# Attention stage of a four-layer pipeline: row sums from the exponentials' accumulator output, and weighing in pairs of rows

## The chip, the cores and the metric

The kernel runs on one core of one Trainium2 chip. The core has five engines, each with a queue of its own that runs in order: TensorE (PE in the profile; PEld is its weight load), VectorE (DVE), ScalarE (ACT), GpSimd (POOL) and SyncE (SP, which here only starts transfers). They meet at semaphores alone. The metric is the time of one execution on the device in microseconds.

## The reference

The input is x, an image of 256 rows x 256 columns x 128 channels. Four layers follow, each with a group normalization ahead. Only the first, attention along each row of the image, is touched:

```
q = split_heads(gn(x) @ Wq) / sqrt(32);  k, v = split_heads(kv_x @ Wk), split_heads(kv_x @ Wv)
a = softmax(einsum('bnhqc,bnhkc->bnhqk', q, k) + mask_bias + tri_bias)      # 4 heads of 32 channels
o = einsum('bnhqk,bnhkc->bnhqc', a, v) * sigmoid(gn(x) @ Wg)
x = x + o @ Wo
```

Here n is the image row, and q and k run over its 256 columns. So there are 256 independent attentions, each with 4 heads and scores of 256 x 256. A Fourier layer, a convolution layer and a gated layer with large kernels follow.

## The kernel before

`attention` writes the whole stage as one block with a queue for each engine. All 256 rows are unrolled. In iteration n the queues work on different rows at once, and the order inside an iteration is written out by hand (the loops `for n in range(-2, rows + 2)` at the end of each engine's part). Each buffer is guarded by waits on counting semaphores.

For a row, with its 256 columns as two halves of 128:

- TensorE turns the row's x and kv_x by transposes into `p_in` (`turn`, L328). VectorE reads them out with the normalization applied (`read_turn`, L511, L512).
- TensorE makes queries and keys (`project_qk`, L333, L334), ScalarE reads them (`read_qk`). Then it makes values and gate (`project_vg`, L339, L341), and ScalarE reads the values and the exponential of minus the gate (`read_vg`, L448, L449). All four steps share the one bank `p_in`.
- TensorE makes the scores (`score`, L350), the four heads in four row groups of the array. VectorE adds the bias and finds the maximum (`add_bias`, L478), ScalarE takes the exponentials (`exps`, L427) into `probs`. The bias, `tri` plus the row's mask, is added by GpSimd (`add_mask`, L309).
- The exponentials are turned by 128x128 transposes (`turn_probs`, L361) into two banks. Heads 0 and 2 use `p_t[0]`, which VectorE reads (L486); heads 1 and 3 use `p_t[1]`, which ScalarE reads (L419). Both go to `probs_t`.
- The softmax's denominator is a column sum of the turned exponentials. GpSimd adds the two halves of the keys (`pair`, L301), and TensorE multiplies the result by a matrix of ones, head by head in the four column groups of the array, so that each sum comes out on all 32 channels of its head (L376). The values are weighed in the same column groups (L373). Together they are `weigh`.
- VectorE multiplies the sums by one plus the gate's exponential (`denominator`, L493). ScalarE inverts that by Ln and then Exp of the negative (`invert`, L433, L435). VectorE multiplies it with the weighed values (`gate`, L500), TensorE projects (`project_out`, L383), VectorE adds x (`residual`, L506), and SP stores the row.

`weigh`, `denominator`, `invert`, `gate`, `project_out` and `residual` of row n - 2 run in iteration n, each once a row. On TensorE `weigh` stands between `project_vg(n + 1)` and the transposes of head 0. On VectorE `gate` stands ahead of `add_bias(n + 1, 0)`, and `residual` between `add_bias(n + 1, 1)` and `add_bias(n + 1, 2)`. On ScalarE `invert` stands behind the exponentials of heads 1 to 3.

Of the kernel before, what the change touches and what calls it, by code (L numbers as in the profile page):

```python
# [202 lines left out]
def attention(nc, x, kv, tri_bias, mask_bias, wq, wk, wv, wg, wo, ident, scale, shift, x1, rows=ROWS):  # L203
# [7 lines left out]
    maskv = mask_bias[0].rearrange("r a b k -> r (a b) k")  # L211
    with ExitStack() as ctx:
# [3 lines left out]
        ones = m.sb("ones", [128, HEAD_DIM])  # L216
# [3 lines left out]
        xs = m.sb("xs", [128, 8, HALVES, CH])  # L220
        kvs = m.sb("kvs", [128, 8, HALVES, CH])
# [4 lines left out]
        vs = m.sb("vs", [128, 4, HALVES, CH])  # L226
        gate_e = m.sb("gate_e", [128, 4, COLS])
        den = m.sb("den", [128, 2, COLS])
# [3 lines left out]
        probs_t = m.sb("probs_t", [128, 3, HEADS, HALVES, COLS])  # L232
        paired_t = m.sb("paired_t", [128, 2, HEADS, COLS])
        og = m.sb("og", [128, 2, COLS])
# [7 lines left out]
        const_loaded, cleared = m.sem("const_loaded"), m.sem("cleared")  # L242
        x_loaded = [m.sem(f"x_loaded{i}") for i in range(8)]
        kv_loaded = [m.sem(f"kv_loaded{i}") for i in range(8)]
        mask_loaded = [m.sem(f"mask_loaded{i}") for i in range(4)]
        x1_stored = [m.sem(f"x1_stored{i}") for i in range(4)]
# [3 lines left out]
        p_turned, even_read, odd_read, paired = (m.sem(n) for n in ("p_turned", "even_read", "odd_read", "paired"))  # L250
        weighed, den_made, den_step, gated = (m.sem(n) for n in ("weighed", "den_made", "den_step", "gated"))
# [5 lines left out]

        @block.sync
        def _(sp):
            def load(n):  # L260
                if n >= 8:
                    sp.wait_ge(x1_made, n - 7)
                    sp.wait_ge(turned, n - 7)
                sp.dma_start(xs[:, n % 8], xv[n]).then_inc(x_loaded[n % 8], 16)
                sp.dma_start(kvs[:, n % 8], kvv[n]).then_inc(kv_loaded[n % 8], 16)
# [13 lines left out]
            for n in range(-2, rows + 2):  # L279
                if n + 4 < rows:  # L280
                    load(n + 4)
                if n + 4 < rows:
                    load_mask(n + 4)
                if exists(n - 2):
                    sp.wait_ge(x1_made, n - 1)
                    sp.dma_start(x1v[n - 2], x1s[:, (n - 2) % 4]).then_inc(x1_stored[(n - 2) % 4], 16)
            for p in range(4):
                sp.wait_ge(x1_stored[p], 16 * (rows // 4))

        @block.gpsimd  # L290
        def _(pool):
            pool.memset(ones[:, :], 1.0).then_inc(cleared, 1)
            pool.wait_ge(const_loaded, 16 * 6)

            def pair(n, half):
                pool.wait_ge(even_read, 2 * n + half + 1)
                pool.wait_ge(odd_read, 2 * n + half + 1)
                if n >= 2:
                    pool.wait_ge(weighed, n - 1)
                part = slice(2 * half, 2 * half + 2)  # L300
                pool.tensor_tensor(paired_t[:, n % 2, part], probs_t[:, n % 3, part, 0], probs_t[:, n % 3, part, 1],  # L301
                                   ALU.add).then_inc(paired, 1)
# [9 lines left out]
            for n in range(-2, rows + 2):  # L312
                for half in range(2):
                    if exists(n - 1):
                        pair(n - 1, half)
                    if exists(n + 2):
                        add_mask(n + 2, half)

        @block.tensor
        def _(pe):  # L320
            def turn(n):
                pe.wait_ge(x_loaded[n % 8], 16 * (n // 8 + 1))
                pe.wait_ge(kv_loaded[n % 8], 16 * (n // 8 + 1))
                if n >= 1:
                    pe.wait_ge(vg_read, n)
                for i, src in enumerate((xs, kvs)):
                    for half in range(HALVES):
                        mm = pe.transpose(p_in[:, i, half * 128:(half + 1) * 128], src[:, n % 8, half, :], ident[:, :])  # L328
                mm.then_inc(turned, 1)
# [25 lines left out]
            def turn_probs(n, h):  # L355
                pe.wait_ge(exped, n * HEADS + h + 1)
                if n >= 1 or h >= 2:
                    pe.wait_ge((even_read, odd_read)[h % 2], n * 2 + h // 2)
                for kh in range(HALVES):
                    for qh in range(HALVES):  # L360
                        mm = pe.transpose(p_t[h % 2][:, kh, qh * 128:(qh + 1) * 128],  # L361
                                          probs[:, h, qh, kh * 128:(kh + 1) * 128], ident[:, :])
                mm.then_inc(p_turned, 1)

            def weigh(n):
                pe.wait_ge(paired, 2 * n + 2)
                pe.wait_ge(vg_read, n + 1)
                if n >= 1:
                    pe.wait_ge(x1_made, n)
                for kh in range(HALVES):  # L370
                    for h in range(HEADS):
                        ch = slice(HEAD_DIM * h, HEAD_DIM * (h + 1))
                        pe.matmul(p_out[ch, 0, :], vs[:, n % 4, kh, ch], probs_t[:, n % 3, h, kh, :],  # L373
                                  start=kh == 0, stop=kh == HALVES - 1)
                for h in range(HEADS):
                    mm = pe.matmul(p_out[HEAD_DIM * h:HEAD_DIM * (h + 1), 1, :], ones[:, :], paired_t[:, n % 2, h, :],  # L376
                                   start=True, stop=True)
                mm.then_inc(weighed, 1)

            def project_out(n):  # L380
                pe.wait_ge(gated, n + 1)
                for half in range(HALVES):
                    mm = pe.matmul(p_out[:, 0, half * 128:(half + 1) * 128], og[:, n % 2, half * 128:(half + 1) * 128], wo_s,  # L383
                                   start=True, stop=True)
# [3 lines left out]
            pe.wait_ge(cleared, 1)  # L388
            for n in range(-2, rows + 2):
                if exists(n + 1):  # L390
                    project_vg(n + 1)
                if exists(n - 2):
                    weigh(n - 2)
# [12 lines left out]
                if exists(n - 2):  # L406
                    project_out(n - 2)
                if exists(n):
                    turn_probs(n, 3)

        @block.scalar
        def _(act):
            act.preload_act_table_set(EXP_LN_SET)

            def read_probs(n, h):
                act.wait_ge(p_turned, n * HEADS + h + 1)
                if n >= 3:
                    act.wait_ge(weighed, n - 2)
                act.activation(probs_t[:, n % 3, h], p_t[1][:, :, :], ACT.Copy).then_inc(odd_read, 1)  # L419

            def exps(n, h):
                act.wait_ge(biased, n * HEADS + h + 1)
                if n >= 1:
                    act.wait_ge(p_turned, (n - 1) * HEADS + h + 1)
                for qh in range(HALVES):
                    i = h * HALVES + qh
                    e = act.activation(probs[:, h, qh, :], neg_s[:, n % 2, h, qh, :], ACT.Exp,  # L427
                                       bias=neg_max[:, n % 2, i:i + 1], scale=-1.0)
                e.then_inc(exped, 1)

            def invert(n):
                act.wait_ge(den_made, n + 1)
                act.activation(den[:, n % 2], den[:, n % 2], ACT.Ln).then_inc(den_step, 1)  # L433
                act.wait_ge(den_step, 2 * n + 1)
                act.activation(den[:, n % 2], den[:, n % 2], ACT.Exp, scale=-1.0).then_inc(den_step, 1)  # L435
# [8 lines left out]
            def read_vg(n):  # L444
                act.wait_ge(vg_made, n + 1)
                if n >= 4:
                    act.wait_ge(den_made, n - 3)
                act.activation(vs[:, n % 4], p_in[:, 0, :], ACT.Copy)  # L448
                act.activation(gate_e[:, n % 4], p_in[:, 1, :], ACT.Exp, scale=-1.0).then_inc(vg_read, 1)  # L449

            for n in range(-2, rows + 2):
# [6 lines left out]
                if exists(n - 2):  # L458
                    invert(n - 2)
# [10 lines left out]
        def _(dve):  # L470
# [11 lines left out]
            def read_probs(n, h):  # L482
                dve.wait_ge(p_turned, n * HEADS + h + 1)
                if n >= 3:
                    dve.wait_ge(weighed, n - 2)
                dve.tensor_copy(probs_t[:, n % 3, h], p_t[0][:, :, :]).then_inc(even_read, 1)  # L486

            def denominator(n):
                dve.wait_ge(weighed, n + 1)
                dve.wait_ge(vg_read, n + 1)  # L490
                if n >= 2:
                    dve.wait_ge(gated, n - 1)
                dve.scalar_tensor_tensor(out=den[:, n % 2], in0=gate_e[:, n % 4], scalar=1.0, in1=p_out[:, 1, :],  # L493
                                         op0=ALU.add, op1=ALU.mult).then_inc(den_made, 1)

            def gate(n):
                dve.wait_ge(den_step, 2 * n + 2)
                if n >= 2:
                    dve.wait_ge(out_made, n - 1)
                dve.tensor_tensor(og[:, n % 2], p_out[:, 0, :], den[:, n % 2], ALU.mult).then_inc(gated, 1)  # L500

            def residual(n):
                dve.wait_ge(out_made, n + 1)
                if n >= 4:
                    dve.wait_ge(x1_stored[n % 4], 16 * (n // 4))
                dve.tensor_tensor(x1s[:, n % 4].rearrange("p h c -> p (h c)"), p_out[:, 0, :],  # L506
                                  xs[:, n % 8].rearrange("p h c -> p (h c)"), ALU.add).then_inc(x1_made, 1)
# [6 lines left out]
            for n in range(-2, rows + 2):  # L514
                if exists(n - 2):
                    denominator(n - 2)
# [4 lines left out]
                if exists(n - 2):  # L521
# [1723 lines left out]
```

## Time and profile before

| what | value |
|---|---|
| median of 3 executions | 4797.06 us (4793.52 to 4877.1) |
| profiled execution | 4796.05 us |
| its span, first to last instruction | 4793.8 us |
| mean granted TensorE clock | 0.958 of 2.4 GHz |
| TensorE busy | 4411.2 us, 92% of the span |
| VectorE busy | 3431.3 us, 72% |
| ScalarE busy | 2804.1 us, 58% |
| GpSimd busy | 2614.8 us, 55% |

Attention runs from about 112 to about 1985 us of the span. A row of a timeline gives the start, the time from the start of its first instruction to the end of its last, the engine, the line, the operation, output and inputs by the program's names, and how many instructions were merged in it. A bracket at its end says how long the engine was idle before it and what released it. On TensorE the ends are modelled and neighbours overlap, so the distance from one start to the next tells more than a duration. A matmul of fp32 counts as two instructions. In a row of the table of stretches stand the stretch, its length, the busy time of PE, PEld, DVE, ACT and POOL with their instructions in brackets, the granted TensorE clock as a share of 2.4 GHz, the share of DMA time and GB/s.

### The profile page before, as it was taken

The numbers are of one execution on the slowest core, as the hardware profiler recorded it, in microseconds if no ns is written. First come the engines' busy times: TensorE is split into PE (matmuls) and PEld (weight loads), VectorE is DVE, ScalarE is ACT, GpSimd is POOL, SyncE is SP. The second block draws the span as 40 slices with busy tenths as digits, with TensorE's granted clock in tenths as the row PEclk, the third lists the DMA queues.
The fourth block names the chain that finished last, engine by engine and source line by source line (L and its number), as shares of the span: only waits on it lengthen the run. The fifth ranks groups of instructions, "written<-read, shape, count | busy, mean of one in ns | idle before, by whom it ended". The sixth has DMA issues, their size and how long they took to land. (4 is left out here: it accounts for less than half of the span.)

```text
span 4793.8 us, 108030 instructions
## 1 busy us (share of the span) xinstructions
PE 4411.2 (92%) x36006; PEld 3297.2 (69%) x36006; DVE 3431.3 (72%) x10053; ACT 2804.1 (58%) x6302; POOL 2614.8 (55%) x2043
## 2 busy tenths in 40 slices
PE   5999999999999999777899989999749997999996
PEld 5777777777777777534577766777424445999995
DVE  7888888888888888651566666666429995567666
ACT  0888888888888888402333343333325662666665
POOL 0999999999999999402233322333105551122222
PEclk8999999999999999887999999999869998999997
DMA  7222222222222222597322222222567887999995
GB/s 311 63 77 73 75 74 74 75 74 76 75 75 75 73 75 74 187 381 248 104 71 73 71 84 71 73 71 73 223 220 214 277 278 245 264 292 293 291 291 137
DMA packets 803939, 713.02 MB, mean 149 GB/s; under 512 B 60693, under 2 KB 700948, under 8 KB 794839
## 3 DMA queue, kind: packets, MB, share of 16 engines
q1 hardware_dynamic: 784875, 672.74, 45.8%
q10 hardware_dynamic: 14717, 20.01, 1.2%
q0 software_dynamic: 3808, 13.47, 0.7%
q8 instruction: 292, 4.78, 0.4%
q14 instruction: 247, 2.02, 0.1%
HBM read 506.70 MB, written 199.29 MB: 147 GB/s over the span
## 5 line engine op out<-in xcount | busy, mean ns | idle before, releaser
L309 POOL TENSOR_TENSOR at_bias<-at_tri,at_mask 128x1024 f32<-128x1024 f32 x512 | 1216.0, 2375 | 27.9 <-DMA at_mask<-in_L_conv_mask_bias_dram 12.1
L427 ACT ACTIVATE at_probs<-at_neg_s,at_neg_max 128x256 f32<-128x256 f32 x2048 | 871.4, 505 | 0.7 <-DVE at_neg_max L478 0.7
L478 DVE CUSTOM_DVE_ANT_0 at_neg_s<-at_p_s,at_bias 128x256 f32<-128x256 f32 x2048 | 759.8, 418 | 7.6 <-PE at_p_s L350 2.9
L301 POOL TENSOR_TENSOR at_paired_t<-at_probs_t 128x512 f32<-128x512 f32 x512 | 655.9, 1281 | 9.7 <-ACT at_probs_t L419 5.6
L361 PE MATMUL at_p_t<-all_ident,at_probs 128*128 128x128 f32 x4096 | 628.3, 276 | 0.6 <-DVE at_probs_t L486 0.4
L969 ACT ACTIVATE ml_h<-ml_p_turns,l_b 128x512 f32<-128x512 f32 x384 | 263.8, 687 | 607.2 <-PE ml_p_turns L928 607.2
L361 PEld LDWEIGHTS at_p_t<-all_ident,at_probs 128*128 128x128 f32 x4096 | 476.0, 141 | 131.7 <-issue 104.1
L1070 POOL TENSOR_TENSOR ml_x2t<-ml_z,ml_xb 128x512 f32<-128x512 f32 x128 | 163.7, 1279 | 675.1 <-DVE ml_z L1036 675.1
L937 PEld LDWEIGHTS ml_p<-l_w1s,ml_h 128*128 128x128 f32 x4096 | 471.9, 192 | 52.7 <-issue 52.7
L1990 POOL TENSOR_TENSOR dw_room<-dw_room,all_b_plain 128x512 f32<-128x512 f32 x128 | 176.9, 1382 | 589.1 <-DMA dw_room<-x3t 589.1
L928 PE MATMUL ml_p_turns<-ml_h,l_w 128*128 128x512 f32 x1024 | 485.3, 597 | 2.3 <-DVE ml_h L1002 2.3
L937 PE MATMUL ml_p<-l_w1s,ml_h 128*128 128x128 f32 x4096 | 484.6, 277 | 0.8 <-issue 0.8
L486 DVE COPY at_probs_t<-at_p_t 128x512 f32<-128x512 f32 x512 | 352.6, 689 | 36.0 <-PE at_p_t L361 1.5
L2023 DVE SCALAR_TENSOR_TENSOR dw_hid<-dw_room 128x512 f32<-128x512 f32 x128 | 154.4, 1206 | 207.8 <-ACT dw_room L1919 207.8
L419 ACT ACTIVATE at_probs_t<-at_p_t 128x512 f32<-128x512 f32 x512 | 300.2, 586 | 1.2 <-PE at_p_t L361 1.2
L350 PE MATMUL at_p_s<-at_keys,at_queries 32*128 32x256 f32 x4096 | 294.3, 401 | 0.0
L373 PE MATMUL at_p_out<-at_probs_t,at_vs 128*32 128x256 f32 x4096 | 274.2, 385 | 1.4 <-DVE at_x1s L506 1.4
L1008 DVE TENSOR_SCALAR ml_h<-ml_p_turns,l_b 128x512 f32<-128x512 f32 x128 | 96.0, 750 | 244.4 <-PE ml_p L937 242.0
L928 PEld LDWEIGHTS ml_p_turns<-ml_h,l_w 128*128 128x128 f32 x1024 | 176.2, 192 | 132.4 <-issue 127.6
L1817 PE MATMUL dw_p_conv<-dw_xw,all_kept 128*128 128x128 f32 x2048 | 253.4, 276 | 9.9 <-DMA dw_xw<-planes 5.8
L1817 PEld LDWEIGHTS dw_p_conv<-dw_xw,all_kept 128*128 128x128 f32 x2048 | 244.3, 192 | 10.5 <-DMA dw_xw<-planes 5.9
L1817 PE MATMUL dw_p_conv<-dw_xw,dw_wts 128*128 128x128 f32 x2048 | 250.8, 274 | 0.0
(230 smaller groups left out, 9110.2 us busy)
## 6 DMA issues: line engine op xcount, KB each, us to landing
dw_xw<-planes SPq DMA_DIRECT2D x128, 528.0 KB, 4.7
sp_xs<-x SPq DMA_DIRECT2D x128, 512.0 KB, 9.1
dw_wts<-patch_w SPq DMA_DIRECT2D x128, 512.0 KB, 6.2
planes<-pw_plane SPq DMA_DIRECT2D x128, 264.0 KB, 3.2
in_xs<-in_x_dram SPq DMA_DIRECT2D x32, 1024.0 KB, 7.7
at_xs<-in_x_dram SPq DMA_DIRECT2D x256, 128.0 KB, 2.5
at_kvs<-in_L_conv_kv_x_dram SPq DMA_DIRECT2D x256, 128.0 KB, 2.7
at_mask<-in_L_conv_mask_bias_dram SPq DMA_DIRECT2D x256, 128.0 KB, 3.3
```

What stands on the lines that cost most here:

```text
L301: pool.tensor_tensor(paired_t[:, n % 2, part], probs_t[:, n % 3, part, 0], probs_t[:, n % 3, part, 1], ALU.add).then_inc(paired, 1)
L309: pool.tensor_tensor(bias[:, n % 2, part], tri[:, part], mask[:, n % 4].unsqueeze(1).broadcast_to((128, 4, COLS)), ALU.add).then_inc(maske ...
L350: mm = pe.matmul(p_s[h][:, qh, :], queries[ch, n % 2, qh * 128:(qh + 1) * 128], keys[ch, n % 2, :], start=True, stop=True)
L361: mm = pe.transpose(p_t[h % 2][:, kh, qh * 128:(qh + 1) * 128], probs[:, h, qh, kh * 128:(kh + 1) * 128], ident[:, :])
L373: pe.matmul(p_out[ch, 0, :], vs[:, n % 4, kh, ch], probs_t[:, n % 3, h, kh, :], start=kh == 0, stop=kh == HALVES - 1)
L419: act.activation(probs_t[:, n % 3, h], p_t[1][:, :, :], ACT.Copy).then_inc(odd_read, 1)
L427: e = act.activation(probs[:, h, qh, :], neg_s[:, n % 2, h, qh, :], ACT.Exp, bias=neg_max[:, n % 2, i:i + 1], scale=-1.0)
L478: t = dve.tensor_tensor_reduce(neg_s[:, n % 2, h, qh, :], p_s[h][:, qh, :], bias[:, n % 2, i, :], -1.0, 3.0e38, ALU.add, ALU.min, neg_max[ ...
L486: dve.tensor_copy(probs_t[:, n % 3, h], p_t[0][:, :, :]).then_inc(even_read, 1)
L928: mm = pe.matmul(bank_of(hidden_use(t, b))[:, :], w0[:, b * 128:(b + 1) * 128], h[:, t % 2, :], start=True, stop=True)
L937: mm = pe.matmul(p_2[:, j, :], h1[:, b, j * 128:(j + 1) * 128], w1c[:, b, :], start=b == 0, stop=b == blocks - 1)
L1817: mm = pe.matmul(p_conv[g % 2][:, j, :], weights, xw[:, k % 3, :, g % 2 * 4 + j, side:side + PX], start=side == 0, stop=side == 1)
```

## The change

- The exponentials get an accumulator output, which leaves each query's sum in `sums` (queries on partitions). GpSimd spreads a row's sums over the 32 channels of each head (`spread_sums`), and for two rows at a time TensorE transposes them (`turn_sums`) into `p_t[0]`. `pair`, `paired_t`, `ones` and the ones matmuls go.
- `weigh`, `denominator`, `invert`, `gate`, `project_out` and `residual` handle two rows q = (2q, 2q + 1) in one visit. `pair_at(n, lag)` gives the pair that is due in iteration n: the denominator, weighing, inversion and gate at lag 3 (odd n), the output projection and the residual at lag 4 (even n), the store at lag 5, `turn_sums` at lag 2 (even n).
- `p_out` holds weighed values of two rows in its two halves. Buffers get deeper: `xs` and `kvs` 10 rows, `vs` and `gate_e` 6, `probs_t` 4, `den` and `og` two pairs.

```diff
+    held, pairs = 10, rows // 2
...
+        def pair_at(n, lag):
+            return (n - lag) // 2 if n % 2 == lag % 2 and lag <= n < rows + lag else None
...  gpsimd
-            def pair(n, half):
-                ...
-                pool.tensor_tensor(paired_t[:, n % 2, part], probs_t[:, n % 3, part, 0], probs_t[:, n % 3, part, 1],
-                                   ALU.add).then_inc(paired, 1)
+            def spread_sums(n):
+                pool.wait_ge(exped, (n + 1) * HEADS)
+                if n >= 4:
+                    pool.wait_ge(sums_turned, (n - 4) // 2 + 1)
+                pool.tensor_copy(spread[:, n % 4], sums[:, n % 4].unsqueeze(3).broadcast_to((128, HALVES, HEADS, HEAD_DIM))
+                                 ).then_inc(sums_spread, 1)
...
             for n in range(-2, rows + 2):
-                for half in range(2):
-                    if exists(n - 1):
-                        pair(n - 1, half)
-                    if exists(n + 2):
-                        add_mask(n + 2, half)
+                if exists(n + 2):
+                    add_mask(n + 2, 0)
+                if exists(n - 1):
+                    spread_sums(n - 1)
+                if exists(n + 2):
+                    add_mask(n + 2, 1)
...  tensor, turn_probs
+                if h == 0 and n >= 3:
+                    pe.wait_ge(den_made, (n - 1) // 2)
...
+            def turn_sums(q):
+                pe.wait_ge(sums_spread, 2 * q + 2)
+                pe.wait_ge(even_read, min(4 * q + 6, 2 * rows))
+                for r in range(2):
+                    for half in range(HALVES):
+                        mm = pe.transpose(p_t[0][:, r, half * 128:(half + 1) * 128],
+                                          spread[:, (2 * q + r) % 4, half].rearrange("p h d -> p (h d)"), ident[:, :])
+                mm.then_inc(sums_turned, 1)
+
+            def weigh(q):
+                pe.wait_ge(even_read, 4 * q + 4)
+                pe.wait_ge(odd_read, 4 * q + 4)
+                pe.wait_ge(vg_read, 2 * q + 2)
+                if q >= 1:
+                    pe.wait_ge(x1_made, q)
+                for r in range(2):
+                    n = 2 * q + r
+                    for kh in range(HALVES):
+                        for h in range(HEADS):
+                            ch = slice(HEAD_DIM * h, HEAD_DIM * (h + 1))
+                            mm = pe.matmul(p_out[ch, r, :], vs[:, n % 6, kh, ch], probs_t[:, n % 4, h, kh, :],
+                                           start=kh == 0, stop=kh == HALVES - 1)
                 mm.then_inc(weighed, 1)
...
-            for n in range(-2, rows + 2):
+            for n in range(-2, rows + 3):
                 if exists(n + 1):
                     project_vg(n + 1)
-                if exists(n - 2):
-                    weigh(n - 2)
+                q = pair_at(n, 3)
+                if q is not None:
+                    weigh(q)
                 if exists(n):
                     turn_probs(n, 0)
...
                 if exists(n):
                     turn_probs(n, 2)
-                if exists(n - 2):
-                    project_out(n - 2)
+                q = pair_at(n, 4)
+                if q is not None:
+                    project_out(q)
                 if exists(n):
                     turn_probs(n, 3)
+                q = pair_at(n, 2)
+                if q is not None:
+                    turn_sums(q)
...  scalar, exps
                     e = act.activation(probs[:, h, qh, :], neg_s[:, n % 2, h, qh, :], ACT.Exp,
-                                       bias=neg_max[:, n % 2, i:i + 1], scale=-1.0)
+                                       bias=neg_max[:, n % 2, i:i + 1], scale=-1.0,
+                                       accum_out=sums[:, n % 4, qh, h:h + 1])
...  vector
+                dve.scalar_tensor_tensor(out=den[:, q % 2], in0=gate_e[:, 2 * q % 6:2 * q % 6 + 2], scalar=1.0, in1=p_t[0][:, :, :],
+                                         op0=ALU.add, op1=ALU.mult).then_inc(den_made, 1)
...
-            for n in range(-2, rows + 2):
-                if exists(n - 2):
-                    denominator(n - 2)
+            for n in range(-2, rows + 3):
+                weighing, leaving = pair_at(n, 3), pair_at(n, 4)
+                if weighing is not None:
+                    denominator(weighing)
                 if exists(n):
                     read_probs(n, 0)
                 if exists(n + 2):
                     read_turn(n + 2)
-                if exists(n - 2):
-                    gate(n - 2)
+                if weighing is not None:
+                    gate(weighing)
                 if exists(n + 1):
                     add_bias(n + 1, 0)
                     add_bias(n + 1, 1)
-                if exists(n - 2):
-                    residual(n - 2)
+                if leaving is not None:
+                    residual(leaving)
                 if exists(n + 1):
                     add_bias(n + 1, 2)
                 if exists(n):
...
```

In the part of SP, the store of row n - 2 becomes one transfer for a pair at lag 5, with two semaphores in place of four, and a load of row n waits for `x1_made` of the pair of row n - 10.

## Rows read from the trace of the kernel before

**Rows 1.** busy time of each engine (x count), granted clock, 480 to 960 us

```profile
...
480.00:960.00 480.00, 480.00 (x4914) 363.36 (x4913) 405.64 (x1524) 410.87 (x1063) 476.39 (x266) 1.00 0.28 75
...
```

**Rows 2.** timeline of TensorE: start us, duration us, line, tiles, count

```profile
...
1001.81 1.15 PE L350 MATMUL at_p_s<-at_keys,at_queries 32*128 32x256 f32 x16
1002.89 0.70 PE L333 MATMUL at_p_in<-at_xn,at_weights 128*128 128x256 f32 x2
...
1003.86 0.60 PE L361 MATMUL at_p_t<-all_ident,at_probs 128*128 128x128 f32 x4
1004.29 0.61 PE L383 MATMUL at_p_out<-at_weights,at_og 128*128 128x128 f32 x4
1004.74 0.60 PE L361 MATMUL at_p_t<-all_ident,at_probs 128*128 128x128 f32 x4
1005.18 0.61 PE L339 MATMUL at_p_in<-at_weights,at_kvt 128*128 128x128 f32 x4
1005.62 0.60 PE L341 MATMUL at_p_in<-at_xn,at_weights 128*128 128x256 f32 x2
1006.15 1.07 PE L373 MATMUL at_p_out<-at_probs_t,at_vs 128*32 128x256 f32 x16
1007.04 0.61 PE L376 MATMUL at_p_out<-at_paired_t,at_ones 128*32 128x256 f32 x8
1007.59 0.66 PE L361 MATMUL at_p_t<-all_ident,at_probs 128*128 128x128 f32 x4
...
1009.04 1.15 PE L350 MATMUL at_p_s<-at_keys,at_queries 32*128 32x256 f32 x16
...
```

**Rows 3.** GpSimd groups, 600 to 1400 us: busy, mean ns, idle

```profile
...
L301 POOL TENSOR_TENSOR at_paired_t<-at_probs_t 128x512 f32<-128x512 f32 x221 | 283.0, 1280 | 0.0
```

**Rows 4.** timeline of VectorE

```profile
...
1002.86 0.42 DVE L500 TENSOR_TENSOR at_og<-at_p_out,at_den 128x256 f32<-128x256 f32 x1 [0.34 <-ACT at_den L435]
...
1004.94 0.42 DVE L506 TENSOR_TENSOR at_x1s<-at_p_out,at_xs 128x256 f32<-128x256 f32 x1 [0.29 <-PE at_p_out L383]
1005.28 0.41 DVE L478 CUSTOM_DVE_ANT_0 at_neg_s<-at_p_s,at_bias 128x256 f32<-128x256 f32 x1
...
1005.97 0.69 DVE L486 COPY at_probs_t<-at_p_t 128x512 f32<-128x512 f32 x1
...
```

**Rows 5.** timeline of ScalarE

```profile
...
1002.41 0.42 ACT L435 ACTIVATE at_den<-at_den 128x256 f32<-128x256 f32 x1
...
1004.60 0.91 ACT L427 ACTIVATE at_probs<-at_neg_s,at_neg_max 128x256 f32<-128x256 f32 x2
1005.40 0.59 ACT L419 ACTIVATE at_probs_t<-at_p_t 128x512 f32<-128x512 f32 x1
1006.26 0.38 ACT L448 ACTIVATE at_vs<-at_p_in 128x256 f32<-128x256 f32 x1 [0.26 <-PE at_p_in L341]
...
1006.80 2.50 ACT L427 ACTIVATE at_probs<-at_neg_s,at_neg_max 128x256 f32<-128x256 f32 x6
...
```

**Rows 6.** groups by line, whole execution

```profile
...
L478 DVE DVE_READ_ACCUMULATOR2_ANT at_neg_max<- 128x1 f32 x2048 | 170.3, 83 | 0.0
...
L977 ACT ACTIVATE ml_rstd<-ml_rstd 128x4 f32<-128x4 f32 x128 | 26.3, 205 | 4.0
...
```

**Rows 7.** timeline of ScalarE at the start of attention

```profile
...
132.98 2.50 ACT L427 ACTIVATE at_probs<-at_neg_s,at_neg_max 128x256 f32<-128x256 f32 x6
...
139.21 0.91 ACT L427 ACTIVATE at_probs<-at_neg_s,at_neg_max 128x256 f32<-128x256 f32 x2
```

**Rows 8.** timeline of TensorE at the start of attention

```profile
...
133.94 0.66 PE L361 MATMUL at_p_t<-all_ident,at_probs 128*128 128x128 f32 x4
134.53 1.15 PE L350 MATMUL at_p_s<-at_keys,at_queries 32*128 32x256 f32 x16
...
```

**Rows 9.** busy time by stretch, two other stretches

```profile
...
130.00:140.00 10.00, 9.68 (x88) 6.81 (x86) 7.91 (x35) 8.65 (x23) 10.00 (x6) 1.00 0.05 12
2200.00:2300.00 100.00, 72.80 (x388) 63.52 (x388) 28.80 (x51) 30.42 (x69) 34.32 (x64) 0.87 0.56 179
...
```

## What the change is expected to do, written before it ran

> **What bounds the kernel now.** I read first the table of busy time by stretch, to see in which part the changed function runs and which engine is full there. In the row from 480 to 960 us TensorE is busy all the time at the full clock (1.00, which is 2.4 GHz), GpSimd 99%, ScalarE 86%, VectorE 85% [rows 1]. Two engines look full, so shares don't settle it; the order of time does. TensorE's timeline repeats every 7.23 us, once for each row of the image (scores at 1001.81 and 1009.04), and the visits follow one another without a hole: 1.08 for the scores, 0.97 for queries and keys, 0.43 for a head's transposes, 0.45 for the output projection, 0.44 and 0.53 for values and gate, 0.89 for weighing, 0.55 for the column sums [rows 2]. I call the distance from one start to the next a slot. GpSimd's paired sums start without idle time [rows 3], but no engine waits for them, and the sums of a row are weighed one visit later. So TensorE's own work sets the 7.23 us, with GpSimd just under it by coincidence. A pair of rows is 14.46 us.
>
> The second thing to see is how late the other engines run behind TensorE. VectorE's copy of head 2 starts at 1005.97 and lasts 0.69, so it ends at 1006.66 [rows 4], while TensorE transposed that head at 1003.86 [rows 2]. It costs nothing, because TensorE wants that bank next at 1007.59. ScalarE starts the exponentials of heads 1 to 3 only when values and gate of the next row have been read [rows 5].
>
> **What the change takes away on TensorE.** Per pair: two column-sum groups, 2 x 0.55; one of two changes to the column groups, 0.09 (0.53 against 0.44 of the visits before weighing); back comes the return, 0.11, that sat in 0.55 (four groups of 128x256 at 0.11 would be 0.44). It adds four transposes of the spread sums, 0.44 [rows 2]. 14.46 - 1.10 - 0.09 + 0.11 + 0.44 = 13.82 us. If nothing waits, 0.64 x 128 pairs = 82 us are gained. GpSimd loses two 1.28 us additions for each row and gets one copy 256 wide; it falls far below TensorE, and that is worth nothing by itself.
>
> **What it adds on ScalarE.** Each of the eight exponentials of a row gets an accumulator output. The trace has none on ScalarE. VectorE writes one as an instruction of its own, 83 ns [rows 6]; I expect the same form and price here, 8 x 0.083 = 0.66 a row. Lower end: 0, since VectorE's own is hidden in the overlap of its neighbours (0.69 for two operations, rows 4). A gain I exclude, as the exponential itself is unchanged. Upper end: a whole small ACTIVATE, 205 ns [rows 6]. The inversion becomes 512 wide: by the step from the 256-wide read to the 512-wide copy, 0.38 to 0.59, each of Ln and Exp goes from 0.42 (the row of the Exp) to about 0.62 [rows 5]. Total ScalarE work falls short of 14 us a pair, so it isn't full; what counts is where it stands in the chain.
>
> **The new waits.** Two iterations now differ. The even one has the output projection (4 matmuls, 2 x 0.45 = 0.90), the 512-wide residual and, at its end, turn_sums; the odd one has denominator, weighing, inversion and gate. turn_sums writes p_t[0], so it waits until VectorE has read head 2 of the same row; behind it in TensorE's queue stands everything of the next row. VectorE in turn has the residual ahead of that copy, and the residual waits for the output projection. I follow the chain round one pair.
>
> (a) From the even iteration's head 1 to turn_sums. Transposes 0.59 when TensorE had to wait (133.94 to 134.53, rows 8), scores 1.08, queries and keys 0.97, head 2 0.43, output projection 0.90 [rows 2]; until a result is visible 0.20 (slot end 1004.74, residual at 1004.94, rows 2, 4); residual 0.60 (a 512-wide copy lasts 0.69, less the overlap of 0.08 between neighbours), head 2's bias 0.69, its copy 0.69 [rows 4], waking TensorE about 0.1 (after head 1's exponentials, done at 132.98 + 0.40 + 0.50 = 133.88, it was 0.06, rows 7, 8). Sum 6.25. From scores' end to turn_sums this is 4.58, and TensorE's own work there is 0.97 + 0.43 + 0.90 + 0.44 = 2.74: it stands still 1.84 us.
>
> (b) turn_sums 0.44, values and gate 0.97, ScalarE begins 0.11 later (1006.15, 1006.26): 1.52 [rows 2, 5].
>
> (c) ScalarE: reads 0.54; three heads' exponentials 2.40 (2.50 for six, which ends 0.10 past the slot) + 6 x 0.083 = 2.90; Ln and Exp 0.62 + 0.03 + 0.62, gate 0.03 later, as 1002.86 stands behind 1002.41 + 0.42 (I take the same 0.03 between the two): 4.74 [rows 4, 5]. Here nothing covers any more: the next row's VectorE work is queued behind the gate.
>
> (d) VectorE's gate 0.60, bias of head 0 0.77 with its accumulator read; ScalarE: head 0's exponentials 0.80 + 0.17 = 0.97, head 3's copy 0.55, values and gate 0.54, head 1's exponentials 0.91 + 0.17 = 1.08, waking 0.05: 4.56 [rows 4, 5, 7, 8]. The other branch, biases 0 to 2 and the copy of head 2 before TensorE may transpose head 0 of the next even row, gives 0.60 + 2.07 + 0.69 + 0.1 + 0.86 = 4.32 and is just shorter. Before, weighing stood between the gate's read and the next turn in every iteration and covered both; in the even one nothing covers them now.
>
> Round: 6.25 + 1.52 + 4.74 + 4.56 = **17.07 us a pair**, against 14.46. 2.61 x 128 = 334 us. The start of this very stage shows that such rounds bind: the rows that don't weigh yet repeat in 6.23 us (132.98 to 139.21) though TensorE has less than that to do, because the transposes of head 1 wait for the exponentials [rows 7, 8].
>
> The sum is against the profiled execution: 4793.8 span, 4796.05 for the execution, 1 us under the median 4797.06. 4796 + 334 = **5130 us**.
>
> **Edits at nothing.** Loads and stores: a load has some rows' time in a ring of ten; the stores are half as many and twice as large on SP, which has nothing else to do; if that cover failed, TensorE would wait at turn. GpSimd's spread waits for row n - 1's exponentials, done over one row before turn_sums; it would have to be a whole row late. The wait of head 0's transposes for the denominator is covered in the odd iteration by values, gate and weighing (0.97 + 1.9 against 0.2 + 0.7). Three more iterations at the end add a few us at most.
>
> **Bounds of the accumulator read.** Ten of them lie in the round. At 205 ns each: + 1.22, 18.29, 490 us more, 5286. At 0, TensorE's own branch takes over (weighing 1.88, transposes and turn 1.45, scores 1.08, queries and keys 0.97, 0.20; ScalarE 0.54, 0.80, 0.55, 0.54, 0.91, 0.05, which is 8.97 after values and gate): 6.25 + 1.41 + 8.97 = 16.63, 278 us more, 5074.
>
> **The clock.** In rows 1 it is 1.00; where TensorE was busy 73% (2200 to 2300 us) the mean was 0.87 [rows 9], between its two levels of 1.2 and 2.4 GHz. The forecast leaves TensorE busy 13.82 of 17.07, 81%, in pieces with holes of one to two microseconds. I take 1.00, since the start of the stage ran through its short holes at the full clock (1.00 from 130 to 140 us, rows 9). If it fell to 0.87, the 6.4 us of TensorE slots in the round would grow by 0.96: 123 us more, 5253. [...]
>
> **The rivals.**
> 1. The round as above, 5074 to 5286 with its bounds, likeliest 5130: 0.60. For it: each wait is in the code and each duration in a row.
> 2. Only turn_sums waits; ScalarE and VectorE make up the rest, as they have slack on the mean: 13.82 + 1.84 = 15.66, 1.20 x 128 = 154, 4950: 0.14. Against it: ScalarE can't start before values and gate, which stand behind turn_sums.
> 3. Not slower. The mechanism is VectorE's copy of head 2: if it is done when TensorE reaches turn_sums, 13.82 holds, 82 us are gained, 4714. It decides at 2.74 us after the scores' end; my sum says 4.58. For it: TensorE is the full engine now and its work shrinks. With ScalarE's waits partly back it ends within 2%. 0.14.
> 4. The clock falls, 5253: 0.07. A read costlier than my bound: 0.02. A mix of the first three that ends within 2% of before: 0.03.
>
> That the change doesn't do what it says I hold for excluded: the additions, the ones and their matmuls are gone from the code.
>
> **The numbers.** A measurement of this kernel can tell about 2% (96 us) from no change. Case 3's 4714 is itself inside 2%; half of its chance goes to gains over 2% that I can't derive. Faster 0.07; same 0.07 + 0.03 = 0.10; slower 0.60 + 0.14 + 0.07 + 0.02 = 0.83. The range holds cases 1, 2 and half of 4, without the extreme of the accumulator's price: 4930 to 5250. The likeliest case alone: 5074 to 5200.
>
> **What would show it.** In the profile after: a period of two rows of about 17 us; TensorE idle 1.8 us before the transposes of the spread sums, released by VectorE's copy of head 2; a second, shorter hole in the same iteration before head 0's or head 1's transposes; VectorE waiting about 1 us for the output projection before the residual; accumulator reads on ScalarE of about 80 ns, 2048 of them; column-sum groups gone. Wrong would be the forecast if the copy of head 2 came before TensorE is through head 3, or if the period were under 15 us.

## The result, and the profile after

The changed kernel takes 5149.77 us (median of 4 runs, 5146.98 to 5154.11) against 4795.29 before. The ratio is 1.0737, 95% interval [1.0723, 1.0751]. Some executions of these kernels come out about 80 us longer at a lower granted clock (4877.1 us among the four of before), the ratios leave them out, and only the profile of e5 below is of such an execution. The profiled execution of the changed kernel has a span of 5148.3 us, 354.5 more than before.

All of it is in attention. One stretch of it, by engine, to be set against [rows 1]:

```profile
480.00:960.00 480.00, 402.14 (x3772) 304.18 (x3774) 328.99 (x1201) 379.05 (x1278) 282.33 (x168) 1.00 0.24 62
```

TensorE is no longer full: 84% busy, still at the full clock. No engine is full now: ScalarE, the busiest but one, has 79%. When nothing is full and the time has grown, the engines wait for one another in a round, and the timeline shows where. TensorE, one pair of rows (start us, duration, line, tiles, count, and in brackets the idle time before it), against [rows 2]:

```profile
...
1000.19 0.60 PE L347 MATMUL at_p_in<-at_xn,at_weights 128*128 128x256 f32 x2
1001.80 0.63 PE L369 MATMUL at_p_t<-all_ident,at_probs 128*128 128x128 f32 x4 [1.01 <-ACT at_probs L451]
...
1002.89 0.66 PE L369 MATMUL at_p_t<-all_ident,at_probs 128*128 128x128 f32 x4
1003.48 1.15 PE L356 MATMUL at_p_s<-at_keys,at_queries 32*128 32x256 f32 x16
...
1005.96 1.06 PE L401 MATMUL at_p_out<-at_weights,at_og 128*128 128x128 f32 x8
1006.85 0.60 PE L369 MATMUL at_p_t<-all_ident,at_probs 128*128 128x128 f32 x4
1009.17 0.63 PE L378 MATMUL at_p_t<-all_ident,at_spread 128*128 128x128 f32 x4 [1.72 <-DVE at_probs_t L512]
1009.64 0.61 PE L345 MATMUL at_p_in<-at_weights,at_kvt 128*128 128x128 f32 x4
1010.09 0.60 PE L347 MATMUL at_p_in<-at_xn,at_weights 128*128 128x256 f32 x2
1010.62 1.93 PE L393 MATMUL at_p_out<-at_probs_t,at_vs 128*32 128x256 f32 x32
...
1013.94 1.15 PE L356 MATMUL at_p_s<-at_keys,at_queries 32*128 32x256 f32 x16
...
1016.89 0.71 PE L345 MATMUL at_p_in<-at_weights,at_kvt 128*128 128x128 f32 x4
1017.44 0.60 PE L347 MATMUL at_p_in<-at_xn,at_weights 128*128 128x256 f32 x2
```

The gate's matmul of the even iteration starts at 1000.19, and the next one at 1017.44: 17.25 us a pair against 14.46. There are two holes, 1.72 us before turn_sums (L378) and 1.01 before head 0's transposes. VectorE in the same time, against [rows 4]:

```profile
...
1001.01 0.69 DVE L512 COPY at_probs_t<-at_p_t 128x512 f32<-128x512 f32 x1
...
1007.05 0.69 DVE L534 TENSOR_TENSOR at_x1s<-at_p_out,at_xs 128x512 f32<-128x512 f32 x1 [0.94 <-PE at_p_out L401]
...
1008.34 0.68 DVE L512 COPY at_probs_t<-at_p_t 128x512 f32<-128x512 f32 x1
...
1015.59 0.69 DVE L527 TENSOR_TENSOR at_og<-at_p_out,at_den 128x512 f32<-128x512 f32 x1 [0.95 <-issue]
...
```

The residual (L534) waits 0.94 us for the output projection, the copy of head 2 behind it ends at 1009.02, and turn_sums starts at 1009.17. The profile puts the other hole down to ScalarE's exponentials. The times say something else: head 0's exponentials ended at 1000.84 (L451 below), VectorE's copy of head 2 of the row before ended at 1001.70, and the transposes started at 1001.80. For a wait on several semaphores, compare the ends.

ScalarE, against [rows 5]:

```profile
...
1000.25 0.49 ACT L451 ACTIVATE at_probs<-at_neg_s,at_neg_max 128x256 f32<-128x256 f32 x1
1000.65 0.19 ACT L451 ACTIVATION_READ_ACCUMULATOR at_probs<-at_neg_s,at_neg_max 128x1 f32 x1
...
1010.72 0.38 ACT L473 ACTIVATE at_vs<-at_p_in 128x256 f32<-128x256 f32 x1 [2.63 <-PE at_p_in L347]
...
1011.27 0.51 ACT L451 ACTIVATE at_probs<-at_neg_s,at_neg_max 128x256 f32<-128x256 f32 x1
1011.66 0.20 ACT L451 ACTIVATION_READ_ACCUMULATOR at_probs<-at_neg_s,at_neg_max 128x1 f32 x1
1011.76 0.51 ACT L451 ACTIVATE at_probs<-at_neg_s,at_neg_max 128x256 f32<-128x256 f32 x1
...
1014.22 0.62 ACT L458 ACTIVATE at_den<-at_den 128x512 f32<-128x512 f32 x1
1014.87 0.63 ACT L460 ACTIVATE at_den<-at_den 128x512 f32<-128x512 f32 x1
...
1016.46 0.38 ACT L467 ACTIVATE at_keys<-at_p_in 128x256 f32<-128x256 f32 x1
...
```

The accumulator output is an instruction of its own, 196 ns long over all 2048. It overlaps the next exponential: exponentials start 0.49 us apart (1011.27, 1011.76, with the read between) and not 0.40. So its price, where exponentials follow one another, is 0.09, and its duration misleads. And ScalarE stands idle for 2.63 us before the values: TensorE, which holds the matmul that ScalarE needs, itself waits at turn_sums.

### The profile page after: what moved, and what is told of

It is laid out like the page before. It is cut to its first block and busy times, and to the rows that moved or that the text cites. A ratio compares the mean times of both kernels' runs of the same rounds, so it can differ in the third digit from the quotient of the medians.

```text
span 5148.3 us, 105458 instructions
## 1 busy us (share of the span) xinstructions
PE 4416.1 (86%) x34470; PEld 3303.9 (64%) x34470; DVE 3377.7 (66%) x9669; ACT 2969.2 (58%) x8094; POOL 2066.0 (40%) x1786
## 5 line engine op out<-in xcount | busy, mean ns | idle before, releaser
L451 ACT ACTIVATE at_probs<-at_neg_s,at_neg_max 128x256 f32<-128x256 f32 x2048 | 1013.9, 504 | 20.9 <-DVE at_neg_max L504 20.9
L369 PE MATMUL at_p_t<-all_ident,at_probs 128*128 128x128 f32 x4096 | 611.6, 277 | 133.5 <-ACT at_probs L451 128.7
L369 PEld LDWEIGHTS at_p_t<-all_ident,at_probs 128*128 128x128 f32 x4096 | 465.2, 141 | 289.8 <-ACT at_probs L451 262.8
L451 ACT ACTIVATION_READ_ACCUMULATOR at_probs<-at_neg_s,at_neg_max 128x1 f32 x2048 | 401.1, 196 | 0.0
L356 PE MATMUL at_p_s<-at_keys,at_queries 32*128 32x256 f32 x4096 | 294.2, 401 | 0.0
L473 ACT ACTIVATE at_vs<-at_p_in 128x256 f32<-128x256 f32 x256 | 96.3, 376 | 334.1 <-PE at_p_in L347 334.1
L378 PE MATMUL at_p_t<-all_ident,at_spread 128*128 128x128 f32 x512 | 80.3, 279 | 218.3 <-DVE at_probs_t L512 218.3
```

The costliest lines, as they stand in the source:

```text
L356: mm = pe.matmul(p_s[h][:, qh, :], queries[ch, n % 2, qh * 128:(qh + 1) * 128], keys[ch, n % 2, :], start=True, stop=True)
```

## The experiments

Theory A is the round of the prediction. Theory B is that ScalarE's added reads are what costs. Theory C is that the wait of turn_sums is the whole loss. Periods below are taken from the start of one scores group (L356) to the next one of the same parity.

**e1, the residual behind the copy of head 2.**

```diff
-                if leaving is not None:
-                    residual(leaving)
                 if exists(n + 1):
                     add_bias(n + 1, 2)
                 if exists(n):
                     read_probs(n, 2)
+                if leaving is not None:
+                    residual(leaving)
```

> The changed kernel with one edit: VectorE's residual of a pair stands behind the copy of head 2 instead of ahead of it. Theory A (a round of waits through all engines sets the pair's 17.25 us): the copy is then done 2.9 us after the scores' end and not 4.6, the hole of 1.7 us before turn_sums goes, the rest of the round stays: 15.5 us a pair, 220 us less than the changed kernel, about 4930. Theory B (ScalarE's added accumulator reads are what costs): the residual is not on ScalarE, so nothing moves, 5150. Theory C (turn_sums' wait is the whole loss): all is back, 4795 or less.

Measured: 4946.95 us, ratio to before 1.0362 [1.0289, 1.0435], 15.62 us a pair. TensorE in this kernel:

```profile
...
1003.25 0.60 PE L369 MATMUL at_p_t<-all_ident,at_probs 128*128 128x128 f32 x4
1003.94 0.63 PE L378 MATMUL at_p_t<-all_ident,at_spread 128*128 128x128 f32 x4
...
1008.71 1.15 PE L356 MATMUL at_p_s<-at_keys,at_queries 32*128 32x256 f32 x16
...
1013.81 0.63 PE L369 MATMUL at_p_t<-all_ident,at_probs 128*128 128x128 f32 x4 [1.01 <-ACT at_probs L451]
...
```

Head 3's transposes take 0.44, so 0.25 us of the 1.88 before turn_sums are left (the copy of head 2 now ends at 1003.80), and the other hole is untouched. B is out for this part, as nothing on ScalarE was changed. C is out too: 152 us are left.

**e2, the gate behind the copy of head 2.** `gate(weighing)` moves from ahead of `add_bias(n + 1, 0)` to ahead of `add_bias(n + 1, 3)`.

> The changed kernel with one edit: VectorE's gate stands behind the copy of head 2 in the odd iteration instead of ahead of the bias of head 0. Theory A: the branch through inversion and gate gets 1 us shorter, but the branch through ScalarE (queries and keys, exponentials of head 0, copy of head 3, values and gate, exponentials of head 1) is nearly as long and takes over: only 0.2 to 0.3 us a pair, 35 us less than the changed kernel, about 5115. If the wait for the inversion were a loss of its own, 1 us a pair would come back, about 5020. Theories B and C: 5150.

Measured: 5109.16 us, ratio 1.0652 [1.0631, 1.0674], 16.99 us a pair. TensorE:

```profile
...
1003.26 0.41 PE L334 MATMUL at_p_in<-all_ident,at_xs 128*128 128x128 f32 x2 [0.40 <-ACT at_gate_e L474]
...
1004.15 0.66 PE L369 MATMUL at_p_t<-all_ident,at_probs 128*128 128x128 f32 x4 [0.25 <-ACT at_probs L451]
...
```

The hole before head 0 is gone. In its place come 0.40 before the turn and 0.25 before head 1, both released by ScalarE: the second branch. Taking away a wait of 1 us gave 0.26.

**e3, both moves.**

> Both moves, residual and gate behind the copy of head 2. Theory A: the two act in different iterations and add up, 15.25 us a pair, about 4895, still slower than before, because in the even iteration nothing on TensorE covers ScalarE's way from values and gate to the exponentials of head 1. Theory B: 5150. Theory C: 4795 or less.

Measured: 4905.22 us, ratio 1.0234 [1.0217, 1.0251], 15.35 us a pair. The two savings, 1.63 and 0.26, add up to 1.9, as expected of waits in different parts of one round.

**e4, no accumulator output.** `accum_out` is left out and the sums are a constant, so this kernel leaves out the softmax's denominator.

> The changed kernel without the accumulator output: the exponentials write no sums, and the sums are a constant 256 set once, so the softmax's denominator is left out of the computation. All visits and waits stay. Theory A: ten of sixteen reads of 0.09 us lie in the round, of which the other branches take part back: 0.6 us a pair, about 5070. Theory B: the whole added time comes back, at least 16 x 0.093 = 1.5 us a pair, 4960 or less. Theory C: 5150.

Measured: 5072.06 us, ratio 1.0577 [1.0559, 1.0595], 16.69 us a pair. 0.56 us a pair came back, not 1.5: B is wrong as the main cause and right for a fifth of the loss (78 of 354 us).

**e5, the kernel before plus the accumulator output.**

```diff
                     e = act.activation(probs[:, h, qh, :], neg_s[:, n % 2, h, qh, :], ACT.Exp,
-                                       bias=neg_max[:, n % 2, i:i + 1], scale=-1.0)
+                                       bias=neg_max[:, n % 2, i:i + 1], scale=-1.0,
+                                       accum_out=sums[:, n % 4, qh, h:h + 1])
```

> The kernel before with the accumulator output added to the exponentials; nothing reads the sums, everything else stays as before. Theory A: 8 x 0.093 = 0.74 us more a row on ScalarE, of which it idles 1.0; the round through inversion and gate gets 0.56 longer and had 0.9 to spare. So nothing or nearly nothing: 4795, at most 4810. Theory B (the added reads cost what they last): 0.74 x 256 = 190 us more, 4985.

Measured: 4797.09 us, ratio 1.0002 [0.9993, 1.0011]. The same 2048 reads cost nothing here. What its waits show (engine, line, waited for: us in total from 600 to 1400 us, times, longest):

```profile
DVE at_og L502 <- ACT at_den L437: 97.9, 110, 0.9
...
ACT at_queries L443 <- PE at_p_in L335: 21.1, 110, 0.2
...
```

VectorE now waits 0.9 us for the inversion and not 0.34, and ScalarE's idle time before the queries falls from 0.75 (at_queries, 82.4 us in 110 waits before) to 0.2. TensorE waits for neither, and a row still takes 7.23 us.

**e6, turn_sums behind values and gate.**

```diff
                 if q is not None:
+                    turn_sums(q)
                     weigh(q)
...
-                q = pair_at(n, 2)
-                if q is not None:
-                    turn_sums(q)
```

> The changed kernel with one edit: turn_sums stands behind values and gate of the odd iteration, just ahead of weighing, not ahead of them. Theory A: ScalarE's exponentials of the odd row no longer hang behind the copy of head 2; the copy of head 2 still holds turn_sums for about 0.9 us. 16.0 us a pair, about 4990. If the order of the two visits did not matter, as the same work stands behind the same wait, 5150.

Measured: 4995.85 us, ratio 1.042 [1.0404, 1.0435], 16.11 us a pair. turn_sums still waits 0.84 for the copy of head 2, but ScalarE has its values by then. 154 us came back by swapping two visits behind which the same work stands: the order matters because one of them feeds another engine. Of the 1.14 us a pair, 0.88 come back between the scores of the even iteration and those of the odd one. The other 0.26 come back in the other half, where the hole before head 0 is gone and waits of 0.36 and 0.26 for ScalarE stand in its place, as in e2.

**e7, four moves.** turn_sums as in e6. `project_out` from behind head 2's transposes to ahead of head 0's, where it covers ScalarE's reads in the iteration that doesn't weigh. `residual` ahead of `add_bias(n + 1, 0)`. `gate` between `add_bias(n + 1, 1)` and `add_bias(n + 1, 2)`.

> The changed kernel with four moves: turn_sums behind values and gate; the output projection ahead of head 0's transposes of the even iteration, where it covers ScalarE's reads as weighing does in the odd one; the residual ahead of the bias of head 0, where VectorE is idle; the gate between the biases of head 1 and 2. Theory A: the round shrinks to 14.3 us a pair, set by ScalarE's way in the even iteration: 0.15 us a pair under before, about 4775. If every iteration without weighing costs its 1.0 us whatever covers it: 4905.

Measured: 4795.21 us, ratio 0.9998 [0.9989, 1.0007], 14.47 us a pair. 355 us are back by order alone, with every operation of the change in place. It is 0.15 us a pair short of the expectation.

**e8, the same with head 3 of odd rows copied by VectorE.**

```diff
-                if exists(n):
+                if exists(n) and n % 2 == 0:
                     read_probs(n, 3)
...
+                if exists(n) and n % 2:
+                    dve.wait_ge(p_turned, n * HEADS + 4)
+                    dve.tensor_copy(probs_t[:, n % 4, 3], p_t[1][:, :, :]).then_inc(odd_read, 1)
```

> The kernel of the four moves, and VectorE instead of ScalarE copies head 3 of the odd rows. Theory A: this takes 0.5 us out of ScalarE's way in the round, and TensorE's own work (13.8 us a pair and some tenths of waits) is the bound: 13.95 us a pair, about 4730. If VectorE's copy is late in its turn: 4775 to 4830.

Measured: 4794.23 us, ratio 0.9995 [0.9986, 1.0004]. A miss by 64 us. From the scores of the odd iteration to those of the even one it takes 6.41 us (e7: 6.52), and from there to those of the next odd one 8.06 (e7: 7.95). What one half of the pair gained, the other gave back:

```profile
...
1009.84 0.68 DVE L532 TENSOR_TENSOR at_x1s<-at_p_out,at_xs 128x512 f32<-128x512 f32 x1
1010.44 0.41 DVE L502 CUSTOM_DVE_ANT_0 at_neg_s<-at_p_s,at_bias 128x256 f32<-128x256 f32 x1
...
1012.50 0.68 DVE L510 COPY at_probs_t<-at_p_t 128x512 f32<-128x512 f32 x1
...
```

The scores had been done at about 1010.2; the residual holds the bias back, and with it the copy of head 2 (end 1013.18) and turn_sums (1013.33).

**e9, e8 with the residual behind the copy of head 2.**

> The kernel before this one (four moves and head 3 of odd rows on VectorE) repeated in 14.4 us a pair, not 13.95: its trace shows VectorE's residual (1009.84 to 1010.44) pushing the biases back by 0.2 and a hole of 0.2 us before turn_sums behind it. Here the residual stands behind the copy of head 2. Theory A: the hole goes, 0.2 to 0.25 us a pair, 30 us: about 4765, the first version clearly under before. If the hole is only handed on (weighing now waits for the residual): 4790.

Measured: 4786.77 us, ratio 0.9971 [0.9959, 0.9983], 14.40 us a pair. It is 12 us under the 4799.31 of before measured beside it, 0.3%: far inside 2%, but with an interval that stays under 1. The expectation was 30 us under e8, and it came out at 7. The half that weighs got only 0.07 shorter (8.06 to 7.99). turn_sums still starts about 0.15 us behind the end of the copy of head 2 (1008.14 behind 1008.00), and weighing now starts as much behind the end of the residual (1008.74 behind 1008.59): in part the wait was handed on, as the expectation's second case had it.

**e10, e9 without the accumulator output.**

> The same without the accumulator output (sums constant, so the softmax's denominator is left out). Theory A: what is left of waiting, 0.1 to 0.2 us before head 1's transposes of the even row, goes: 13.98 us a pair, about 4740. Theory B: ScalarE is the engine that bounds by now, so the whole 1.5 us of reads a pair come back as far as TensorE's own work of 13.9 allows: the same 4740; if less than 10 us come back, the reads are hidden here too.

Measured: 4763.78 us, ratio 0.9926 [0.9911, 0.9941], 14.23 us a pair. Like e4, this kernel leaves out the denominator. The reads cost 23 us here (4786.77 - 4763.78), which is 0.17 us a pair, and all of it lies in the half without weighing (6.23 us, e9: 6.41). The half with weighing takes 7.99 in both. TensorE's timeline has no bracket any more, but set beside the other engines it still waits:

```profile
...
1007.15 1.15 PE L357 MATMUL at_p_s<-at_keys,at_queries 32*128 32x256 f32 x16
...
1010.10 0.71 PE L346 MATMUL at_p_in<-at_weights,at_kvt 128*128 128x128 f32 x4
1010.65 0.60 PE L348 MATMUL at_p_in<-at_xn,at_weights 128*128 128x256 f32 x2
1011.21 0.63 PE L379 MATMUL at_p_t<-all_ident,at_spread 128*128 128x128 f32 x4
1011.81 1.93 PE L394 MATMUL at_p_out<-at_probs_t,at_vs 128*32 128x256 f32 x32
...
1015.14 1.15 PE L357 MATMUL at_p_s<-at_keys,at_queries 32*128 32x256 f32 x16
...
```

ScalarE and VectorE in the same time:

```profile
...
1009.67 0.38 ACT L465 ACTIVATE at_keys<-at_p_in 128x256 f32<-128x256 f32 x1
...
1010.38 0.69 DVE L510 COPY at_probs_t<-at_p_t 128x512 f32<-128x512 f32 x1
1010.99 0.68 DVE L532 TENSOR_TENSOR at_x1s<-at_p_out,at_xs 128x512 f32<-128x512 f32 x1
...
```

The values start 0.05 us behind the end of ScalarE's reading of the keys (1010.05), for which `project_vg` waits. turn_sums starts about 0.15 behind the end of VectorE's copy of head 2 (1011.07), just as in the changed kernel (1009.17 behind 1009.02). Weighing starts about 0.15 behind the end of the residual (1011.67). So the half with weighing is still a chain over two engines: scores, VectorE's biases, copy and residual, then weighing, transposes and the next scores.

Values, gate and turn_sums take 0.55 + 0.56 + 0.60 = 1.71 us here. In the changed kernel, where turn_sums comes first, they take 0.47 + 0.45 + 0.53 = 1.45 (1009.17 to 1010.62). The 0.26 between the two is these waits: 0.10 at the values, 0.13 before turn_sums (the gate's slot is 0.43) and 0.04 before weighing (0.60 and not 0.56, as in e7). They are no price of the order on TensorE alone. e7 to e9 have the same distances at the values and at turn_sums (e7: the copy ends at 1011.68, turn_sums starts at 1011.82), which is part of what they fell short. Whether TensorE could go round in the 13.9 us of my expectation, no run shows.

## Why the prediction was right

5130 was forecast, 5150 measured, and the waits are the ones that were forecast. The round, step by step, in the trace after:

| part of the round | forecast us | measured us | from, to |
|---|---|---|---|
| (a) head 1 of the even row to turn_sums | 6.25 | 6.28 | 1002.89, 1009.17 |
| (b) to ScalarE's reading of the values | 1.52 | 1.55 | 1010.72 |
| (c) to VectorE's gate | 4.74 | 4.87 | 1015.59 |
| (d) to head 1 of the next even row | 4.56 | 4.55 | 17.25 less the three above |
| a pair | 17.07 | 17.25 | |

2.79 us more a pair x 128 is 357 us, against 354.5 more in the span. The 3 us between the two are all that falls outside the steady rounds.

- *The wait of turn_sums*, forecast 1.84 us from slot end to start, with the residual waiting for the output projection "about 1 us": 1.88 (1.72 in the bracket) and 0.94 in the trace. TensorE woke 0.15 us behind the end of the copy, where I had taken 0.1. e1 shows that this wait is a cause and what it is worth.
- *The second hole in the even iteration*: there (1.01). I had the branch over ScalarE as the longer one by 0.24. In the trace the copy of head 2 lets head 0's transposes go at 1001.80, and head 1's follow at 1002.89, about 0.2 later than the visits before them need; ScalarE's exponentials of head 1 end at 1002.84. e2 shows both branches: without the first, the second holds.
- *The accumulator's price*: 83 ns taken, a slot of 0.09 measured. That it would be a separate instruction was right; my upper bound of 205 ns would have been wrong for a reason worth keeping, since the row does last 196 ns. e4 gives 78 us for it in the round, where the forecast's own step from 5130 to the lower bound 5074 gave 56. The lower bound itself, 16.63 us a pair with TensorE's own branch taking over, is what e4 measured: 16.69 and 5072.06 us. In its trace head 0's exponentials (1020.18) follow ScalarE's reading of the keys (1019.91) without a gap, and no longer wait for the bias behind VectorE's gate.
- *Part (c)* was 0.13 short: 2.95 for the exponentials instead of 2.90, 1.28 for Ln and Exp instead of 1.27, and the gate 0.09 after the Exp, not 0.03.
- *Part (d)* is right to 0.01 partly by luck: head 3's copy took 0.48 and not 0.55 and the reads of values and gate 0.52 and not 0.54, which made up for exponentials, gate and bias, each 0.01 to 0.03 longer than forecast.
- *TensorE's own work*, 13.82: the changed kernel's period less its holes (1.18, 0.2 and 1.88 from slot end to start) is 13.99. The 0.17 is waiting too, as far as the rows tell. In the odd iteration the values start 0.05 behind ScalarE's reading of the keys (1016.84, 1016.89), 0.03 late, and take 0.55 where I had counted 0.44; head 1's transposes behind their wait take 0.59 and not 0.53. So nothing here speaks against 13.82, and no run shows it either: the shortest period measured is 14.23.
- *GpSimd's relief is worth nothing*: its busy time fell by a fifth (2614.8 to 2066.0 us), and the time grew all the same.

The rivals. "Only turn_sums waits" would give 15.66 us a pair: the trace has 17.25 and a second hole, and e1 and e3, with nearly all of that wait gone, take 4947 and 4905 us, not 4795. "Not slower" needed the copy of head 2 within 2.74 us of the scores' end (1004.55): it ended 4.47 later, at 1009.02. The granted clock stayed at 1.00 through holes of up to 1.9 us with TensorE 84% busy (480 to 960 us), so the rival of the clock is out in this case.

Not tried: turn_sums into a bank of its own, which would need a ninth bank beside the eight that the kernel allocates; and weighing split over both iterations.

## What to carry to other kernels

Batching two units into every second iteration takes the cover away from the iteration that is left without them. Before doing it, list for each hand-over in that iteration what stood beside it, and look in the timeline of before how long after the producer the consumer comes: the copy of head 2 ended 1.5 us after TensorE was through with head 3's transposes (1006.66 and 1005.18, [rows 4] and [rows 2]), and this was invisible as long as nothing needed the bank there.

When an order goes wrong like this, sum the round through all engines in both directions before moving one thing: single moves here were worth 0.26 to 1.63 us of 2.79, four together all of it.

An engine without a bracket in its timeline is not yet an engine that never waits. Where it starts at the same short distance behind another engine's end in every round, as TensorE does in e10, it is released there, and its time is not its own minimum.

## What was unexpected of the hardware

- ScalarE's accumulator read lasts 196 ns in the trace and takes 0.09 us of the engine's time between two exponentials. VectorE's lasts 83 ns and takes none: two bias operations with their reads take 0.69, and the residual of the same size, which has no read, takes 0.34 ([rows 4]).
- A short wait cost TensorE more than its length. The same four matmuls of the values take a slot of 0.45 us where they don't wait (1009.64 to 1010.09 in the changed kernel) and 0.55 where ScalarE's reading of the keys releases them (1016.89 to 1017.44). There they start only 0.03 us late: two heads' transposes and the wait take 0.91 (1015.98 to 1016.89), where twice 0.44 would be 0.88. The weight loads (PEld) show the difference: the first starts 0.11 us ahead of its matmul in the one case (1009.53 and 1009.64) and together with it in the other (1016.89).

```profile
...
1009.53 0.53 PEld L345 LDWEIGHTS at_p_in<-at_weights,at_kvt 128*128 128x128 f32 x4
...
1016.89 0.52 PEld L345 LDWEIGHTS at_p_in<-at_weights,at_kvt 128*128 128x128 f32 x4
...
```

- TensorE's matmuls start about 0.15 us behind the end of the VectorE operation that releases them (turn_sums in the changed kernel and e10, weighing in e9 and e10), and 0.05 us behind the end of ScalarE's reading of the keys.
